# Four message-passing layers on one core: edge tiles of 128 in place of 125, and fewer near tiles

## The chip, the cores and the metric

The kernel runs on one core of a Trainium2 chip. Its time is the device time of one execution in microseconds. A core has five engines that matter here: TensorE (PE; its weight loads are listed apart as PEld), VectorE (DVE), ScalarE (ACT), GpSimd (POOL), and SyncE (SP), which issues most of the transfers. They run their own instruction streams and meet by semaphores.

## The reference

The graph has 3125 nodes with 16 features and 100,000 edges, sorted by destination. Four layers follow each other; each takes h = relu(layernorm(x)) and adds its result to x:

```
L0:  w_edge = relu(edge_attr_16 @ W1 + b1) @ W2 + b2        (16 x 16 per edge)
     msg = h[src] @ w_edge; out = relu(batchnorm(sum over dst + h @ root + bias))
L1:  msg = silu(sum_ij h[dst]_i * edge_attr_8_j * W[i,j,:]) @ W_lin, summed over src,
     then a second tensor product with the node's own features
L2:  two relational convolutions: msg = (h[src] @ W[edge_type]) / count(dst, edge_type),
     summed over dst; then log_softmax
L3:  out = in_degree^-1/2 * sum over dst of (h * out_degree^-1/2)[src]
```

Everything is float32. The kernel carries a float32 value through bfloat16 matmuls as three bfloat16 parts whose sum is the value.

## The kernel before

**Tiling.** Edges lie on partitions. A tile is EP = 125 edges, one on each of 125 partitions; T = 8 tiles are a chunk, and 100 chunks are all edges. Edge number p * 800 + c * 8 + t is partition p, chunk c, tile t, so each load of a chunk takes one piece of consecutive values per partition. Five phases run over all chunks in turn: l0, l1, l2a, l2b and l3, with short stages on the nodes between them. Chunks alternate between two buffers (s = 0, 1).

**Summing by node.** A chunk's messages are summed over their target node by matmuls into one accumulator `acc` [128, 392] that stays in PSUM for the whole phase. The target number is split in a high part (392 values) and a low part (8). DVE and ACT make a one-hot row of 392 for each edge (`one_hot`, L1206 on DVE, L866 and L879 on ACT), and DVE multiplies the three parts of the message by the one-hot of the low part (`stationary`, L1234). L600 is the matmul: 3 parts for 8 tiles, 24 per chunk. In l1 eight more (L607) count out-degrees, in l0 eight more (L604) count edges by node and type.

**Far and near tiles.** The message of an edge needs a row of its other node. For most tiles of a chunk, the far ones, GpSimd gathers these rows from a table in HBM: one indirect DMA per tile (L584), each with 125 row numbers, into `gathered`. The last tiles of a chunk, the near ones, get them without a gather. The node rows lie in SBUF as three bfloat16 parts on 125 partitions of 25 nodes each (`node_parts`). DVE makes a one-hot of the partition for each near edge (L1300, from `near_key`, which SyncE broadcasts to 125 partitions, L443), PE multiplies (L757, six matmuls per tile, 13 and 12 nodes wide), and DVE halves the row of 25 nodes four times by conditional copies (L1321) until one node's row is left. In l1 and l2 DVE then forms the outer product with the edge attributes or the type's one-hot (L1355), PE turns it (L765), ACT copies it (L979), and PE multiplies it by the weights (L773). `NEAR_OF` gives the near tiles of a chunk: none in l0, 3 in l1, 4 in l2a, l2b and l3. The far tiles are the rest of the eight: 8, 5, 4, 4, 4.

In l1 a far tile costs DVE a product of its 128-wide table row with the edge attributes (L1434) and three folds (L1432, L1445). The near tiles' edge attributes are loaded once in l0, for all chunks (`near_ea8`, L509, 1.17 MB in pieces of 96 bytes); the far tiles' come per chunk (`ea8`, L471).

**Order.** Every engine's order is written out by hand. For a chunk of a near phase DVE does the chunk's body (up to `stationary`), then `is_lo` of the next (L1187), then `near_finish` of the chunk after that, with the key comparisons of the third inside it. PE does 12 of its 24 sums, turns the outer product of two chunks ahead, 6 sums, the near rows of three chunks ahead, 6 sums, and the messages of two ahead; in l3 the near rows come after all sums. POOL starts the gathers of a chunk when its row numbers have arrived and DVE has read the rows of two chunks before (L577, L580). SP loads row numbers when the gathers of two chunks before have landed (L430), and the fields when ACT's distances and DVE's last use of two chunks before are done (L464, L465), then the near keys of two chunks ahead (L474).

**Start.** SP loads the edge lists src, dst and type (L376 to L378, 390 KB each), DVE and ACT make eight integer fields per edge from them, and SP stores them to HBM (L408, 3 MB), from where each phase reads them back by chunk.

Of the kernel before, what the change touches and what calls it, by code (L numbers as in the profile page):

```python
# [27 lines left out]
LO = 8  # L28
# [26 lines left out]
def build(nc, A, out):  # L55
    with ExitStack() as ctx:
# [161 lines left out]
        counts = ctx.enter_context(nc.psum_tensor("counts", [128, HI], F32))  # L218
        eaT_ps = ctx.enter_context(nc.psum_tensor("eaT_ps", [128, T, EP + 1], BF16))
        rows_ps = ctx.enter_context(nc.psum_tensor("rows_ps", [128, 3, 512], F32))  # L220
# [144 lines left out]
        WIDE_BANKS = (2, 3, 0)  # L365

        block = ctx.enter_context(nc.Block())


        @block.sync  # L370
        def _(sp):

            sp.wait_ge(ev("x_cleared"), 1)
            for p, l, n in as_nodes:
                sp.dma_start(x[p, l, :], A["x"][n].rearrange("(p l) f -> p l f", l=l.stop)).then_inc(ev("x_in"), 16)
            sp.dma_start(src[:], A["src"].rearrange("(p t) -> p t", p=EP)).then_inc(ev("edges_in"), 16)  # L376
            sp.dma_start(dst[:], A["dst"].rearrange("(p t) -> p t", p=EP)).then_inc(ev("edges_in"), 16)
            sp.dma_start(typ[:], A["edge_type_8"].rearrange("(p t) -> p t", p=EP)).then_inc(ev("edges_in"), 16)  # L378

# [8 lines left out]

            ea_d = A["edge_attr_16"].rearrange("(p c t) f -> p c (t f)", p=EP, t=T)
            ea8_d = A["edge_attr_8"].rearrange("(p c t) f -> p c (t f)", p=EP, t=T)  # L390
            rows_d = {ph: A[k].rearrange("(p c t) -> p c t", p=EP, t=T) for ph, k in (("l0", "src"), ("l1", "dst"), ("l3", "src"))}

            def load_ea(chunk, s):
                sp.dma_start(ea[:, s].rearrange("p t f -> p (t f)"),
                             ea_d[:, bass.ds(chunk, 1), :].rearrange("p c n -> p (c n)")).then_inc(ea_in[s], 16)

# [28 lines left out]

            def load_numbers(ph, chunk, pair, s):

                if later(chunk, 2):

                    sp.wait_ge(S[ph]["rows_in"][s], 16 * far(ph, s) * pair)  # L430
                if ph in rows_d:
                    rows = rows_d[ph][:, bass.ds(chunk, 1), :]
                else:
                    rows = meta_d[:, bass.ds(chunk, 1), SRC_KEY * T:(SRC_KEY + 1) * T]
                sp.dma_start(row_numbers[:, s, :], rows.rearrange("p c n -> p (c n)")).then_inc(numbers_in[s], 16)

            def load_near_keys(ph, chunk, s):
# [5 lines left out]
                sp.dma_start(near_key[:, s, 0:n], near_key_d[bass.ds(chunk, 1), at:at + n].to_broadcast([NEAR_NP, n])  # L443
                             ).then_inc(near_key_in[s], 16)

            def load_near_nodes(ph, into):
# [12 lines left out]
            def stream_near(ph):  # L459
                def body(chunk, pair, s):  # L460
                    load_numbers(ph, chunk, pair, s)
                    if later(chunk, 2):

                        sp.wait_ge(distances_ready, before(ph) + chunk - 1)  # L464
                        sp.wait_ge(S[ph]["step"], done(ph, FIELDS_READ[ph], chunk - 2))  # L465

                        sp.sem_inc(ev("chunks_begun"), 1)
                    sp.dma_start(fields[:, s].rearrange("p k t -> p (k t)"),
                                 meta_d[:, bass.ds(chunk, 1), :].rearrange("p c n -> p (c n)")).then_inc(fields_in[s], 16)
                    if ph == "l1":  # L470
                        sp.dma_start(ea8[:, s].rearrange("p t f -> p (t f)"),  # L471
                                     ea8_d[:, bass.ds(chunk, 1), :].rearrange("p c n -> p (c n)")).then_inc(ea8_in[s], 16)
                    if follows(chunk, 2):
                        load_near_keys(ph, chunk + 2, s)  # L474
                near_chunks(sp, body)

            def stream_l0():
                ph = "l0"

                def body(chunk, pair, s):  # L480
                    if later(chunk, 2):
                        load_numbers(ph, chunk, pair, s)

                        sp.wait_ge(ea_split, 2 * (chunk - 2) + 1)
                        load_ea(chunk, s)
# [29 lines left out]
                with sp.Fori((2 + LO) // 2, PAIRS) as pair:  # L515
                    for s in range(2):
                        body(2 * pair + s, pair, s)

# [76 lines left out]
        def _(pe):  # L595
# [147 lines left out]
            turn_h("l1")  # L743
            pe.wait_ge(ev("diagonals_in"), 16 * (8 * LO + 4))
            wide("l1", "msg")
# [97 lines left out]
        def _(act):  # L843
# [59 lines left out]

            act.wait_ge(ev("edges_in"), 48)
            act.copy(fields_all[:, :, TYPE, :].bitcast(F32), typ[:].rearrange("p (c t) -> p c t", t=T)
# [151 lines left out]
        def _(dve):  # L1057
# [49 lines left out]

            dve.wait_ge(ev("edges_in"), 48)
            for n in range(2):
# [23 lines left out]

            dve.wait_ge(ev("edges_in"), 48)

# [170 lines left out]
            def near_finish(ph, chunk, pair, s, following=True):  # L1306
# [43 lines left out]
                if ph == "l1":  # L1350
                    dve.tensor_copy(near_inverse[:, s, 0:count], rows[:, :, 0, F:ROW1])
                    factor = near_ea8[:, bass.ds(chunk, 1), :].rearrange("p c (t r) -> p (c t) r", t=NEAR1)[:, NEAR1 - count:]
                else:
# [240 lines left out]
```

## Time and profile before

| | |
|---|---|
| median of 3 runs | 4559.57 us (4553.13 to 4559.76) |
| the profiled execution | 4555.6 us, its span 4553.4 us |
| PE | 4339.6 us busy, 95% |
| PEld | 3261.8 us, 72% |
| DVE | 4121.4 us, 91% |
| ACT | 3235.6 us, 71% |
| POOL | 3284.9 us, 72% |
| DMA queues, share of 16 engines | GpSimd's 10.1%, SyncE's 7.8% |

Busy times are unions over the span of one execution. The end of a matmul is modelled, so a busy PE is not one at its peak. A gather's time on POOL ends when the transfer has been handed over, not when the rows have landed. "Issue" as what ended an idle time means that the engine waited for nothing that the profile shows.

### The profile page before, as it was taken

How to read it: one execution, taken by the hardware profiler on the slowest of the kernel's cores; microseconds unless marked ns; L12 is line 12 of the kernel's file. 1: busy time of each engine (PE TensorE's matmuls, PEld its weight loads, DVE VectorE, ACT ScalarE, POOL GpSimd, SP SyncE). 2: the span in 40 equal slices, each digit the busy share in tenths (PEclk: the TensorE clock that was granted, in tenths of full speed). 3: DMA queues.
4: the chain of work that ended last, by engine and by line, in shares of the span. 5: the costliest groups of instructions: out<-in, count | busy, mean ns of one | idle time of the engine just before them, and what ended most of it. 6: DMA issues, size and time to landing. Idle time of an engine off the chain costs nothing.

```text
span 4553.4 us, 107759 instructions
## 1 busy us (share of the span) xinstructions
PE 4339.6 (95%) x30477; PEld 3261.8 (72%) x30477; DVE 4121.4 (91%) x11864; ACT 3235.6 (71%) x5359; POOL 3284.9 (72%) x2515
## 2 busy tenths in 40 slices
PE   4999999999997999999979999998999999799998
PEld 3777777777775777777747777776777777566665
DVE  5999999999997999999969999997999998888887
ACT  3777777777774777777737777775777777677776
POOL 4888888888883777777727777775777775688886
PEclk8999999999998999999989999999999999899999
DMA  3111111111111222222211111111111111111111
GB/s 72 21 17 18 17 18 17 18 18 18 18 17 40 61 59 61 59 60 60 59 37 27 27 28 27 27 28 39 27 28 28 26 28 23 30 31 31 30 31 24
DMA packets 336556, 148.67 MB, mean 33 GB/s; under 512 B 250040, under 2 KB 322532, under 8 KB 336392
## 3 DMA queue, kind: packets, MB, share of 16 engines
q0 software_dynamic: 104000, 59.31, 10.1%
q1 hardware_dynamic: 232517, 88.88, 7.8%
q8 instruction: 19, 0.31, 0.0%
q14 instruction: 20, 0.16, 0.0%
HBM read 135.45 MB, written 9.80 MB: 32 GB/s over the span
## 4 chain that ended last, share of the span: by engine, by line
PE 81%; DVE 10%; issue 5%; ACT 2%; DMA 1%; SPq 1%; DVEq 0%; POOL 0%; POOLq 0%; ACTq 0%
PE acc L600 37%; PE rows_ps L757 16%; PE rows_ps L693 7%; PE bank L773 5%; PE bank L693 4%; PE counts L607 3%; PE eaT_ps L765 3%; DVE raw L1258 2%; PE rows_ps L681 2%; DVE stationary L1234 2%; PE eaT_ps L669 1%; DVE one_hot L1206 1%; PE counts L604 1%; DVE rows_ps L1321 1%; ACT stack L928 1%
## 5 line engine op out<-in xcount | busy, mean ns | idle before, releaser
L600 PE MATMUL acc<-one_hot,stationary 125*128 125x392 bf16 x12000 | 2335.4, 329 | 39.5 <-DVE stationary L1234 35.1
L584 POOL DMA_INDIRECT gathered<-table_l,row_numbers x1200 | 1607.3, 1339 | 461.1 <-issue 349.1
L600 PEld LDWEIGHTS acc<-one_hot,stationary 125*128 125x128 bf16 x12000 | 1157.3, 100 | 709.0 <-DVE stationary L1234 49.9
L866 ACT ACTIVATE distances<-count_hi,fields 125x392 bf16<-125x392 f16 (+1 forms) x2500 | 1227.5, 560 | 0.0
L1234 DVE TENSOR_TENSOR stationary<-mask,parts 125x1024 bf16<-125x1024 bf16 x1500 | 943.3, 683 | 0.3 <-ACT mask L851 0.2
L851 ACT CAST mask<-is_lo 125x1024 bf16<-125x1024 f32 x500 | 523.1, 1046 | 447.3 <-DVE is_lo L1187 393.5
L584 POOL DMA_INDIRECT fields_all<-table_l,row_numbers x500 | 646.3, 1293 | 259.6 <-issue 114.8
L1206 DVE TENSOR_SCALAR one_hot<-count_hi,fields 125x392 bf16<-125x392 f16 x2300 | 734.4, 341 | 13.5 <-issue 13.5
L1321 DVE COPY_PREDICATED rows_ps<-near_bits_now,rows_ps 125x320 f32<-125x320 int8 (+3 forms) x1600 | 579.7, 362 | 162.6 <-PE rows_ps L757 118.6
L584 POOL DMA_INDIRECT gathered<-table_l2a,row_numbers x400 | 512.7, 1282 | 282.6 <-DVE parts L1216 119.4
L757 PE MATMUL rows_ps<-node_parts,h1T 125*125 125x192 bf16 (+1 forms) x7200 | 678.3, 252 | 27.0 <-DVE node_parts L1285 19.6
L757 PEld LDWEIGHTS rows_ps<-node_parts,h1T 125*125 125x125 bf16 x7200 | 660.8, 138 | 56.0 <-DVE node_parts L1285 19.8
L584 POOL DMA_INDIRECT gathered<-table_l2b,row_numbers x400 | 512.6, 1282 | 242.0 <-DVE parts L1216 119.2
L879 ACT ACTIVATE one_hot<-distances,ones 125x1568 bf16<-125x1568 bf16 (+1 forms) x400 | 675.0, 1687 | 6.6
L979 ACT COPY h1T<-eaT_ps 128x500 f32<-128x500 f32 (+1 forms) x300 | 162.7, 542 | 431.5 <-PE eaT_ps L765 431.5
L1258 DVE TENSOR_REDUCE raw<-product 125x32 f32<-125x512 f32 x400 | 395.6, 1010 | 0.0
L693 PE MATMUL rows_ps<-w,h1T 128*125 128x256 f32 x1600 | 385.9, 384 | 9.7 <-DVE product L1251 8.1
L693 PE MATMUL bank<-w,h1T 128*125 128x256 f32 x1600 | 379.7, 380 | 0.0
L693 PEld LDWEIGHTS rows_ps<-w,h1T 128*125 128x125 f32 x1600 | 294.7, 189 | 59.1 <-DVE product L1251 9.5
L693 PEld LDWEIGHTS bank<-w,h1T 128*125 128x125 f32 x1600 | 302.0, 189 | 45.8
L1300 DVE TENSOR_SCALAR h1T<-near_key,node_key 125x500 bf16<-125x500 f16 (+1 forms) x800 | 319.3, 400 | 12.3 <-DMA near_key<-near_keys_by_chunk 12.3
L941 ACT ACTIVATE h1T<-rows_ps,b 128x500 f32<-128x500 f32 x400 | 249.7, 676 | 90.1 <-PE rows_ps L681 90.0
(213 smaller groups left out, 4706.6 us busy)
## 6 DMA issues: line engine op xcount, KB each, us to landing
near_key<-near_keys_by_chunk SPq DMA_DIRECT2D x300, 122.1 KB
gathered<-table_l,row_numbers POOLq DMA_INDIRECT x1200, 2.8
fields<-edge_fields SPq DMA_DIRECT2D x500, 31.2 KB
near_key<-near_keys_by_chunk SPq DMA_DIRECT2D x100, 91.6 KB
fields_all<-table_l,row_numbers POOLq DMA_INDIRECT x500, 3.5
gathered<-table_l2a,row_numbers POOLq DMA_INDIRECT x400
gathered<-table_l2b,row_numbers POOLq DMA_INDIRECT x400
ea<-in_edge_attr SPq DMA_DIRECT2D x100, 62.5 KB
```

Of the source, the lines that this page charges most:

```text
L584: pool.indirect_dma_start(out=gathered[ph][:, s, t, :], in_=table[ph], out_offset=None, in_offset=bass.IndirectOffsetOnAxis(ap=row_numbers ...
L600: mm = pe.matmul(acc[:, :], stationary[:, s, k, t, :, :].rearrange("p a b -> p (a b)"), one_hot[:, s, t, :], start=first and t == 0 and k ...
L693: mm = pe.matmul(bank[2 + q % 2][0:EP, j * HID:(j + 1) * HID], h1T[:, half, t * EP:(t + 1) * EP], w2[:, half, :], start=half == 0, stop=ha ...
L757: mm = pe.matmul(near_rows_ps[ph][:, t, 0:end - first, :].rearrange("p a f -> p (a f)"), near_one_hot[:, g, t * EP:(t + 1) * EP], parts_of ...
L851: act.copy(mask[:, s].rearrange("p t a f -> p (t a) f"), is_lo[:, s].rearrange("p t a -> p (t a)")[:, :, None].to_broadcast([EP, T * LO, F ...
L866: ins = act.activation(distances[:, i * n:(i + 1) * n], count_hi[:, 0:n], ACT.Abs, scale=-1.0, bias=fields[:, s, k, t:t + 1].bitcast(F32))
L879: act.activation(into, distances[:, 0:into.shape[1]], ACT.Relu, scale=-1.0, bias=ones[0:EP, 0:1]).then_inc(scalar_hot, 1)
L1206: dve.tensor_scalar(one_hot[:, s, t, :], count_hi[:, :], scalar_field(s, hi_field[ph], t), None, ALU.is_equal)
L1234: ins = dve.tensor_tensor(stationary[:, s, k], mask[:, s], source[:, s, :, k * F:(k + 1) * F][:, :, None, :].to_broadcast([EP, T, LO, F]), ...
L1258: dve.tensor_reduce(raw[:, s, 2 * q:2 * q + 2, :], product[:, q % 2].rearrange("p t i o -> p t o i"), AX.X, ALU.add).then_inc(products_sum ...
L1300: ins = dve.tensor_scalar(near_one_hot[:, g, 0:n], near_key[:, s, 0:n], node_key[:, g:g + 1], None, ALU.is_equal)
L1321: return dve.copy_predicated(into, chosen, source)
```

## The change

A tile is 128 edges. 100,000 is not a multiple of 1024, so there are 98 chunks, 352 places more than edges. The edges are read through two views that overlap: the first 54 chunks are the first 55,296 edges, partition-major; the last 44 start 352 edges earlier, so that on partition 0 they repeat edges. Those are taken out at the start: on partition 0 DVE sets the source to an unused slot and the destination to a number beyond all one-hots. `near_key` is loaded to 128 partitions and read on 125. `NEAR_OF` becomes 2 in l1, 3 in l2a and l2b, 4 in l3, so the far tiles are 6, 5, 5 and 4. `near_ea8` holds two chunks and is loaded per chunk in l1, behind the near keys and on their semaphore. SP's loops are split where the view changes.

```diff
-EP, T = 125, 8
+EP, T = 128, 8
 E = 100000
-TILES = E // EP
-CHUNKS = TILES // T
+CHUNKS = -(-E // (EP * T))
+TILES = CHUNKS * T
 PAIRS = CHUNKS // 2
-NEAR_OF = {"l0": (0, 0), "l1": (3, 3), "l2a": (4, 4), "l2b": (4, 4), "l3": (4, 4)}
+PADDING = EP * TILES - E
+WHOLE = CHUNKS - PADDING // T
+WHOLE_EDGES = EP * WHOLE * T
+NEAR_OF = {"l0": (0, 0), "l1": (2, 2), "l2a": (3, 3), "l2b": (3, 3), "l3": (4, 4)}
...
-        near_key = sb("near_key", [NEAR_NP, 2, NEARS * EP], F16)
+        near_key = sb("near_key", [128, 2, NEARS * EP], F16)
...
-        near_ea8 = sb("near_ea8", [EP, CHUNKS, NEAR1 * RELATIONS])
+        near_ea8 = sb("near_ea8", [EP, 2, NEAR1, RELATIONS])
...
+        def near_keys_in_by(ph, pair):
+            return 32 * (pair + 1) if ph == "l1" else 16 * (PAIRS + chunks_before(ph) // 2 + pair + 1)
...
+        def by_rows(v):
+            names = "(p c t) f -> p c t f" if len(v.shape) == 2 else "(p c t) -> p c t"
+            return (v[0:WHOLE_EDGES].rearrange(names, p=EP, t=T),
+                    v[WHOLE_EDGES - PADDING:].rearrange(names, p=EP, t=T))
...
+            for into, k in ((src, "src"), (dst, "dst"), (typ, "edge_type_8")):
+                whole, ragged = by_rows(A[k])
+                sp.dma_start(into[:, 0:WHOLE * T], whole.rearrange("p c t -> p (c t)")).then_inc(ev("edges_in"), 16)
+                sp.dma_start(into[:, WHOLE * T:], ragged.rearrange("p c t -> p (c t)")).then_inc(ev("edges_in"), 16)
...
+                if ph == "l1":
+                    if later(chunk, 2):
+                        sp.wait_ge(near_outers, chunk - 1)
+                    sp.dma_start(near_ea8[:, s].rearrange("p t r -> p (t r)"),
+                                 rows_of(ea8_d, chunk, ragged, (T - NEAR1) * RELATIONS)).then_inc(near_key_in[s], 16)
...
-                            sp.dma_start(near_ea8[:], ea8_d[:, :, (T - NEAR1) * RELATIONS:]).then_inc(ev("diagonals_in"), 16)
...
+            dve.memset(src[0:1, WHOLE * T:], SLOTS - 1)
+            link(dve.memset(dst[0:1, WHOLE * T:], SLOTS))
...
-                        dve.wait_ge(near_key_in[s], 16 * (chunks_before(ph) // 2 + pair + 1))
-                    ins = dve.tensor_scalar(near_one_hot[:, g, 0:n], near_key[:, s, 0:n], node_key[:, g:g + 1], None, ALU.is_equal)
+                        dve.wait_ge(near_key_in[s], near_keys_in_by(ph, pair))
+                    ins = dve.tensor_scalar(near_one_hot[:, g, 0:n], near_key[0:NEAR_NP, s, 0:n], node_key[:, g:g + 1], None, ALU.is_equal)
```

## Rows read from the trace of the kernel before

**Rows 1.** Windows in L0, L1, L2a, L3: columns in the first line.

```profile
core 0: us, PE busy (x) PEld busy (x) DVE busy (x) ACT busy (x) POOL busy (x), PEclk, DMA share, GB/s
600.00:1200.00 600.00, 595.06 (x3424) 435.07 (x3423) 579.41 (x1263) 452.72 (x812) 490.04 (x361) 1.00 0.13 18
1500.00:2300.00 800.00, 800.00 (x5557) 605.52 (x5556) 757.32 (x2548) 604.33 (x1038) 610.76 (x472) 1.00 0.27 60
2450.00:3050.00 600.00, 600.00 (x4967) 476.78 (x4966) 559.37 (x1817) 437.08 (x662) 424.23 (x331) 1.00 0.16 27
3950.00:4450.00 500.00, 476.47 (x3737) 345.52 (x3736) 449.46 (x1401) 386.72 (x623) 405.18 (x312) 1.00 0.20 31
```

**Rows 2.** GpSimd's groups, windows L0, L1, L2a, L3: xcount | busy, mean ns | idle before.

```profile
L584 POOL DMA_INDIRECT gathered<-table_l,row_numbers x361 | 491.1, 1360 | 110.0 <-issue 96.6 <-DVE rest L1219 13.1 <-DVE msg L1271 0.3
L584 POOL DMA_INDIRECT fields_all<-table_l,row_numbers x472 | 611.7, 1296 | 189.4 <-issue 107.8 <-DVE parts L1225 74.0 <-DMA row_numbers<-in_dst 7.6
L584 POOL DMA_INDIRECT gathered<-table_l2a,row_numbers x331 | 424.4, 1282 | 176.6 <-DVE parts L1216 101.1 <-issue 62.5 <-DMA row_numbers<-edge_fields 13.1
L584 POOL DMA_INDIRECT gathered<-table_l,row_numbers x312 | 406.3, 1302 | 95.1 <-issue 82.6 <-DVE is_lo L1187 11.9 <-DMA row_numbers<-in_src 0.6
```

**Rows 3.** Chain of waits, L1: start, us, what.

```profile
1492.74 2.29 PE rows_ps L757 x18
1501.23 2.29 PE rows_ps L757 x18
```

**Rows 4.** Timeline of PE, L2a: start, us, what.

```profile
2609.33 0.59 PE L765 MATMUL eaT_ps<-ident,fields_all 125*128 125x125 f32 x4
2616.59 0.59 PE L765 MATMUL eaT_ps<-ident,fields_all 125*128 125x125 f32 x4
```

**Rows 5.** Timeline of GpSimd, L0.

```profile
705.27 1.21 POOL L584 DMA_INDIRECT gathered<-table_l,row_numbers  x1 [0.30 <-issue]
```

**Rows 6.** Waits in the windows of L2a and L3: us in total, times, longest.

```profile
DVE rows_ps L1321 <- PE rows_ps L757: 26.6, 74, 0.5
...
PE acc L600 <- DVE stationary L1234: 23.5, 39, 0.6
```

**Rows 7.** Timeline of PE, L3.

```profile
4107.09 4.15 PE L600 MATMUL acc<-one_hot,stationary 125*128 125x392 bf16 x24 [0.60 <-DVE stationary L1234]
4111.08 2.22 PE L757 MATMUL rows_ps<-node_parts,h1T 125*125 125x208 bf16 x24
```

**Rows 8.** DVE's groups by form, whole span: xcount | busy, mean ns | idle before.

```profile
L1321 DVE COPY_PREDICATED rows_ps<-near_bits_now,rows_ps 125x360 f32<-125x360 int8 x100 | 53.1, 531 | 7.5 <-PE rows_ps L757 7.1 <-ACT near_bits_now L987 0.4
L1321 DVE COPY_PREDICATED rows_ps<-near_bits_now,rows_ps 125x72 f32<-125x72 int8 x100 | 23.8, 238 | 14.5
L1300 DVE TENSOR_SCALAR h1T<-near_key,node_key 125x500 bf16<-125x500 f16 x600 | 252.2, 421 | 8.3 <-DMA near_key<-near_keys_by_chunk 8.3
L1300 DVE TENSOR_SCALAR h1T<-near_key,node_key 125x375 bf16<-125x375 f16 x200 | 67.1, 336 | 4.0 <-DMA near_key<-near_keys_by_chunk 4.0
```

**Rows 9.** DMA queues, windows L2a and L1: packets, MB, share.

```profile
q1 hardware_dynamic: 32370, 13.37, 8.5%
q0 software_dynamic: 10566, 3.03, 7.8%
...
q0 software_dynamic: 37698, 32.62, 18.2%
```

**Rows 10.** SyncE in L1: its longest wait, and its timeline.

```profile
SPq L465 <- ACT distances L866: 557.5, 90, 6.4
...
1698.81 0.26 SPq L443 DMA_DIRECT2D near_key<-near_keys_by_chunk  x1
```

**Rows 11.** Chain of waits, start.

```profile
4.86 16.51 DMA stage<-in_edge_type
...
47.49 11.03 DMA gathered<-table_l,row_numbers
...
74.51 21.58 SPq L511
```

More of the change, by code:

```diff
@@ L387, in _, with rows_of, load_ea @@
                 sp.dma_start(b1[:, a:a + 1], A["L0_gnn_b1"][a * 128:(a + 1) * 128][:, None]).then_inc(ev("w1_in"), 16)
[L389 to L393, printed above, removed]
+            ea_d = [v.rearrange("p c t f -> p c (t f)") for v in by_rows(A["edge_attr_16"])]
+            ea8_d = [v.rearrange("p c t f -> p c (t f)") for v in by_rows(A["edge_attr_8"])]
+            rows_d = {ph: by_rows(A[k]) for ph, k in (("l0", "src"), ("l1", "dst"), ("l3", "src"))}
+            def rows_of(views, chunk, ragged, first=0):
+                view, at = (views[1], chunk - WHOLE) if ragged else (views[0], chunk)
+                return view[:, bass.ds(at, 1), first:].rearrange("p c n -> p (c n)")
+            def load_ea(chunk, s, ragged=False):
                 sp.dma_start(ea[:, s].rearrange("p t f -> p (t f)"),
-                             ea_d[:, bass.ds(chunk, 1), :].rearrange("p c n -> p (c n)")).then_inc(ea_in[s], 16)
+                             rows_of(ea_d, chunk, ragged)).then_inc(ea_in[s], 16)
             for s in range(2):
@@ L424, in later_copies, with load_numbers @@
                     sp.dma_start(bd[k][rows, lo, :, :], A[w].rearrange("r i o -> i r o")).then_inc(ev("diagonals_in"), 16)
-            def load_numbers(ph, chunk, pair, s):
+            def load_numbers(ph, chunk, pair, s, ragged=False):
                 if later(chunk, 2):
@@ L431, in load_numbers, with load_near_keys @@
                 if ph in rows_d:
-                    rows = rows_d[ph][:, bass.ds(chunk, 1), :]
+                    rows = rows_of(rows_d[ph], chunk, ragged)
                 else:
-                    rows = meta_d[:, bass.ds(chunk, 1), SRC_KEY * T:(SRC_KEY + 1) * T]
-                sp.dma_start(row_numbers[:, s, :], rows.rearrange("p c n -> p (c n)")).then_inc(numbers_in[s], 16)
-            def load_near_keys(ph, chunk, s):
+                    rows = meta_d[:, bass.ds(chunk, 1), SRC_KEY * T:(SRC_KEY + 1) * T].rearrange("p c n -> p (c n)")
+                sp.dma_start(row_numbers[:, s, :], rows).then_inc(numbers_in[s], 16)
+            def load_near_keys(ph, chunk, s, ragged=False):
                 if later(chunk, 2) or ph != "l1":
@@ L459, in stream_near, with body @@
             def stream_near(ph):
-                def body(chunk, pair, s):
-                    load_numbers(ph, chunk, pair, s)
+                def body(chunk, pair, s, ragged):
+                    load_numbers(ph, chunk, pair, s, ragged)
                     if later(chunk, 2):
@@ L471, in body @@
                         sp.dma_start(ea8[:, s].rearrange("p t f -> p (t f)"),
-                                     ea8_d[:, bass.ds(chunk, 1), :].rearrange("p c n -> p (c n)")).then_inc(ea8_in[s], 16)
+                                     rows_of(ea8_d, chunk, ragged)).then_inc(ea8_in[s], 16)
                     if follows(chunk, 2):
-                        load_near_keys(ph, chunk + 2, s)
-                near_chunks(sp, body)
+                        load_near_keys(ph, chunk + 2, s, chunk + 2 >= WHOLE if isinstance(chunk, int) else ragged)
+                for chunk in range(2):
+                    body(chunk, 0, chunk, False)
+                with sp.Fori(1, WHOLE // 2 - 1) as pair:
+                    for s in range(2):
+                        body(2 * pair + s, pair, s, False)
+                for chunk in range(WHOLE - 2, WHOLE):
+                    body(chunk, chunk // 2, chunk % 2, False)
+                with sp.Fori(WHOLE // 2, PAIRS - 2) as pair:
+                    for s in range(2):
+                        body(2 * pair + s, pair, s, True)
+                for chunk in range(CHUNKS - 4, CHUNKS):
+                    body(chunk, chunk // 2, chunk % 2, True)
             def stream_l0():
                 ph = "l0"
-                def body(chunk, pair, s):
+                def body(chunk, pair, s, ragged=False):
                     if later(chunk, 2):
-                        load_numbers(ph, chunk, pair, s)
+                        load_numbers(ph, chunk, pair, s, ragged)
                         sp.wait_ge(ea_split, 2 * (chunk - 2) + 1)
-                        load_ea(chunk, s)
+                        load_ea(chunk, s, ragged)
                     if later(chunk, 2):
@@ L514, in stream_l0 @@
                         later_copies(chunk - 2)
-                with sp.Fori((2 + LO) // 2, PAIRS) as pair:
-                    for s in range(2):
-                        body(2 * pair + s, pair, s)
+                for first, end in (((2 + LO) // 2, WHOLE // 2), (WHOLE // 2, PAIRS)):
+                    with sp.Fori(first, end) as pair:
+                        for s in range(2):
+                            body(2 * pair + s, pair, s, end == PAIRS)
             def store_table(ph, stage, where):
@@ L743, in _ @@
             turn_h("l1")
-            pe.wait_ge(ev("diagonals_in"), 16 * (8 * LO + 4))
+            pe.wait_ge(ev("diagonals_in"), 16 * (8 * LO + 3))
             wide("l1", "msg")
@@ L1351, in near_finish @@
                     dve.tensor_copy(near_inverse[:, s, 0:count], rows[:, :, 0, F:ROW1])
-                    factor = near_ea8[:, bass.ds(chunk, 1), :].rearrange("p c (t r) -> p (c t) r", t=NEAR1)[:, NEAR1 - count:]
+                    factor = near_ea8[:, s, NEAR1 - count:]
                 else:
```

14 lines of the change are left out of this document (6 added, 8 removed).

## The prediction

> **What bounds the kernel now.** I read the table of engines first, with one window in each phase [rows 1]. In the tensor-product phase (L1) and the first relational one (L2a; L2b repeats it) TensorE is busy for all of the window and VectorE for 93 to 95%; in L0 PE has 99% and DVE 97%, in the last phase (L3) 95% and 90%. The granted clock is 1.00 in all of them. Then the period of a chunk. From the gathers in a window: 361 of 8 a chunk in 600 us are 13.30 us in L0, 312 of 4 in 500 us are 6.41 in L3 [rows 2]. From equal pieces: 1492.74 and 1501.23 are 8.49 us in L1 [rows 3], 2609.33 and 2616.59 are 7.26 in L2 [rows 4]. One hundred chunks each, L2 twice, are 1330 + 849 + 726 + 726 + 641 = 4272 of the 4555.6 us of the profiled execution; the rest is the start, the node stages and the end.
>
> GpSimd is busy for 71 to 82% of the windows [rows 1] and yet near its limit. After each gather stand 0.30 us that end by nothing: 110.0/361 in L0, 95.1/312 in L3, with 1.36 and 1.30 us for the gather itself. Eight and four of these are 13.3 and 6.4 us, the whole period. In L1 five are 8.0 of 8.49, in L2 four are 6.35 of 7.26, and there GpSimd waits for DVE as well [rows 2]. An undisturbed gather is 1.21 us [rows 5]; what goes beyond comes beside DVE's work. But in L0 and L3 GpSimd is not what others wait for: in L3 the wait of the matmul engine is for DVE's stationary, 23.5 us over 78 chunks, and no gather is in the list [rows 6]. I read L3 as a loop through PE and DVE.
>
> **Chunks.** 800 tiles in 100 chunks become 784 in 98; all that is paid per chunk is paid twice less in each phase. A row of a tile is a partition, so sums, masks and stationaries cost what they did. Columns that count edges grow from 125 to 128, in parts of the chunk only; I count 0 for them and at most 2.4% of the hidden layer's matmuls, under 0.1 us a chunk.
>
> **Near tiles, L1 from 3 to 2, L2 from 4 to 3.** PE: 24 matmuls of the sum take 3.99 us (4107.09 to 4111.08) [rows 7]. So in L2 four near tiles have the other 7.26 - 3.99 = 3.27, each 0.82, and PE needs 6.44 with three. L1 has 32 such matmuls, 5.32, and 3.17 for three near tiles; two leave 7.43.
>
> DVE: a conditional copy costs (531 - 238)/288 = 1.02 ns per element, a key comparison (421 - 336)/125 = 0.68 ns per column [rows 8]. L1 loses 120 + 96 + 48 + 24 elements in its four copies (-0.29), 119 columns in each of two comparisons (-0.16), and 128 elements of the outer product (-0.13, by the same 1.02). It gains one far tile: 128 elements in the product, 64 and 32 in the folds, 16 in the sum, +0.25. Together -0.33. L2 loses 192 elements of copies (-0.20), 116 columns twice (-0.16) and 128 of the outer product (-0.13): -0.49. DVE's own need today: busy 757.3/800 of 8.49 is 8.04 us in L1, 559.4/600 of 7.26 is 6.77 in L2 [rows 1]. In L2 it idles 0.32 us a chunk for PE's rows (26.6 us, 83 chunks [rows 6]), so without PE it needs 6.94, and 6.45 after; I take 6.55, as the loop with PE (6.44) is as long. In L1 it idles 0.45, and I put half on PE: 8.26 - 0.33 = 7.93, taken as 8.0. DVE is late next, PE behind it by 0.1 to 0.6 us. Bounds: today's busy time less the edit, 7.7 and 6.3, and today's period less nothing, 8.49 and 7.26.
>
> **Gathers.** Each near tile less is a gather more: 6 a chunk in L1, 5 in L2. This decides the sign. Means are 1296 and 1282 ns where the undisturbed one is 1.21, so DVE adds 5 x 0.086 = 0.43 and 4 x 0.072 = 0.29 us a chunk [rows 2, 5]; I keep 0.4 and 0.3. At 1.21 us GpSimd would need 6 x 1.515 + 0.4 = 9.49 us in L1 and 5 x 1.515 + 0.3 = 7.88 in L2, above both old periods. What does a gather of 128 rows cost? No row has one, but the queues show how 125 are issued [rows 9]. SyncE's three loads of a chunk in L2 make 32370/83 = 390 packets, 3 x (125 + 5). A gather in L2 moves 3.03 MB/331 = 9154 bytes, of which 125 rows of 64 are 8000. The other 1154 are 288 pieces of 4 bytes: 16 for a semaphore and 272 more, about 11 x 25. In L1 it is 32.62 MB/472 = 69.1 KB for rows of 544 (68.0): the same 1.1 KB. I read it as five DMA engines with 25 rows each and eleven with 25 dummies, some 400 entries for 125 rows. 128 divides by 16, and 16 x 8 = 128 entries do.
>
> The Trainium skill, "DMA: Bandwidth & Descriptors", section "Why a DMA increments its semaphore by 16 and not by 1", has the rule: a DMA uses the largest number of engines up to 16 that divides its slowest dimension, so 5 for 125 and 16 for 128. By that rule, the trace agrees (390 packets).
>
> Bounds of the new gather: 1.21 us if the entries cost nothing (1.24 if time goes with rows), and 1.21 x 8/25 = 0.39 if they are all of it. No row has another count, so I take the middle, 0.8: half of it fixed. Below a threshold the value does not matter: 6 (g + 0.305) + 0.4 reaches 8.0 at g = 0.96, 5 (g + 0.305) + 0.3 reaches 6.55 at 0.945. Up to there DVE sets both phases. That half of the old cost is in the entries is my choice; it is enough that a third is (1.21 x (0.67 + 0.33 x 0.32) = 0.94).
>
> The Trainium skill speaks against so low a value: the section "Latency and other measured facts" of the same page gives about 1 us for what the software path spends on making descriptors. By it, as an estimate from that page, L1 would be 98 x 8.23 and L2 98 x 6.83, and the kernel some 4340 us; the trace's 1.21 stands above the page's figure for 125 rows, and no run here yet shows 128. In rows this is rival B below.
>
> **SyncE.** In L1 the near edge attributes come per chunk now, one issue more of about 0.26 us with a wait on an outer product of two chunks before, long done. The queue waits 557.5/90 = 6.2 us per chunk for ACT's distances, and behind the new issue stand only the row numbers of the next chunk, so I count 0; without that cover it is 98 x 0.26 = 25 us [rows 10]. Loads that now use 16 engines land earlier; in the steady state nobody waits for them.
>
> **Start.** On the chain stand 16.51 us for the edge lists, 11.03 for the first gathers, which share the queues with the 3 MB store of the fields, and 21.58 in which the store of near keys is stuck behind the load of near attributes that the change removes [rows 11]. With an ordinary landing of 2 us left in each, 14 + 9 + 21 = 44 us is the upper bound, 0 the lower (part of each is covered by the node work). I take 25.
>
> **Sum** against 4555.6: L0 2 x 13.30, -27; L1 98 x 8.0 = 784 for 849, -65; L2 98 x 6.55 = 642 for 726, -84 twice; L3 2 x 6.41, -13; start -25. That is -298, 4258. The median of the runs is 4 us above the profiled one: 4262.
>
> **Rivals.** A, slower: the gather stays at 1.21, because its time is fixed and not in the entries. GpSimd then sets L1 (98 x 9.49 = 930, +81) and L2 (98 x 7.88 = 772, +46 twice); less the 65 of L0, L3 and start it is +108, 4668. It turns slower where 588 g - 631 + 980 g - 1094 passes 65, at g = 1.14. For it: rows of 64 and of 544 bytes took the same time. Against it: two thirds of the entries go. Chance 0.13.
> B, between: four fifths fixed, g = 1.05. L1 98 x 8.53 = 836 (-13), L2 98 x 7.08 = 693 (-33 twice), -65: -144, 4416. Chance 0.17.
> C, more: GpSimd's shorter spans disturb DVE less, so the loops of L0 and L3 give half of the 0.30 us that PE waits in L3 (196 x 0.15 = 29) and L1 and L2 0.1 a chunk more (29): 4204. Chance 0.15.
> The forecast has 0.55.
>
> **Range.** 4200 to 4440 holds the forecast, B and C and leaves A out; the forecast's own is 4220 to 4310. Faster by over 0.2% (9 us, about what can be told from no change) 0.86, within it 0.02, slower 0.12, which is nearly all of A.
>
> **What would show it.** A gather under 0.95 us; its queue without the 4-byte dummies; DVE at 97% or more in L1 and L2 and PE idle before DVE's stationary; periods of 8.0 and 6.55, and 13.3 and 6.4 as before in L0 and L3; no 21 us issue at the start. GpSimd without a gap in L1 and L2 and DVE waiting for gathered rows would show A or B. A gather of over 1.0 us makes me wrong.

## The result, and the profile after

The changed kernel took 5332.49 us (median of 4 runs, 5289.03 to 5351.86), beside 4559.65 for the kernel before in the same set of runs: ratio 1.169, 95% interval 1.161 to 1.176, and 25% above the forecast. The profiled execution has 5330.2 us and a span of 5328.3. As the experiments will show, one fact belongs beside it: run again beside a kernel before of 4553.4 us, the same program took 4247.7, ratio 0.932 (0.930 to 0.934). What follows compares these two traces of one program. I call them the long run and the short run.

Windows of the long run, one in each phase (columns as in [rows 1]):

```profile
200.00:1300.00 1100.00, 964.91 (x5401) 694.60 (x5399) 896.04 (x1980) 716.99 (x1280) 587.73 (x568) 0.99 0.09 15
1700.00:2500.00 800.00, 635.23 (x3950) 403.74 (x3948) 628.82 (x2135) 495.45 (x872) 509.14 (x474) 0.97 0.25 55
2750.00:3500.00 750.00, 597.10 (x4087) 418.62 (x4086) 516.07 (x1767) 410.68 (x641) 390.22 (x401) 0.91 0.13 19
4700.00:5200.00 500.00, 422.08 (x3088) 285.79 (x3087) 363.11 (x1161) 320.72 (x518) 265.88 (x257) 0.97 0.15 26
```

Windows of the short run, the same four phases:

```profile
500.00:1100.00 600.00, 587.13 (x3383) 440.06 (x3427) 565.20 (x1262) 455.11 (x812) 374.68 (x362) 1.00 0.11 18
1450.00:2150.00 700.00, 644.55 (x4260) 430.40 (x4258) 664.45 (x2302) 536.26 (x938) 544.20 (x512) 1.00 0.32 68
2300.00:2850.00 550.00, 549.97 (x4326) 411.99 (x4324) 536.14 (x1869) 429.85 (x679) 420.40 (x425) 1.00 0.20 27
3650.00:4150.00 500.00, 495.94 (x3853) 349.92 (x3851) 460.63 (x1448) 398.17 (x644) 330.55 (x322) 1.00 0.20 32
```

The last count before the clock is GpSimd's gathers: 8, 6, 5 and 4 a chunk. So the period of a chunk is 8 x 1100/568 = 15.5 us in L0, 10.1 in L1, 9.35 in L2 and 7.8 in L3 in the long run, and 13.26, 8.20, 6.47 and 6.21 in the short one. In the long run no engine is as full as in the short one (PE has 79 to 88%, GpSimd 52 to 64%), and the granted clock falls to 0.91 in L2. What the engines wait for is seen in the list of waits of the whole span (us in total, times, longest), first the long run:

```profile
DVE rows_ps L1361 <- remote: 616.1, 147, 6.4
...
PEld acc L638 <- issue: 294.5, 1014, 4.5
ACT h1T L1017 <- remote: 253.4, 76, 11.9
...
PE bank L811 <- issue: 190.9, 152, 7.0
```

Of the four the short run has only the second, with 8.0 us; it stands here below that run's largest "remote" wait:

```profile
ACT h1T L979 <- remote: 54.1, 97, 0.6
...
PEld acc L638 <- issue: 8.0, 37, 0.8
```

"Issue" and "remote" mean that no instruction of this core released the one that waits. One such stretch, in the timeline of the long run (start, us, engine, line; rows between these are left out):

```profile
3010.09 1.16 PE L638 MATMUL acc<-one_hot,stationary 128*128 128x392 bf16 x6
3010.36 0.14 SPq L464 DMA_DIRECT2D near_key<-near_keys_by_chunk  x1
3011.18 0.26 DVE L1227 TENSOR_TENSOR is_lo<-count_key,fields 128x64 f32<-128x64 f32 x1
3011.18 0.95 POOL L622 DMA_INDIRECT gathered<-table_l2a,row_numbers  x1 [0.30 <-issue]
3011.81 0.18 PE L811 MATMUL bank<-relation_weights,h1T 128*128 128x16 f32 x1 [0.48 <-issue]
3012.39 0.19 ACT L1025 COPY near_bits_now<-near_bits 128x12 int8 x1
3012.53 0.19 PEld L811 LDWEIGHTS bank<-relation_weights,h1T 128*128 128x128 f32 x1 [1.19 <-issue]
3013.25 0.18 PE L811 MATMUL bank<-relation_weights,h1T 128*128 128x16 f32 x1 [1.26 <-issue]
3013.43 2.15 ACT L904 ACTIVATE distances<-count_hi,fields 128x392 bf16<-128x392 f16 x4
3013.68 0.95 POOL L622 DMA_INDIRECT gathered<-table_l2a,row_numbers  x1 [0.30 <-issue]
3013.96 0.19 PEld L811 LDWEIGHTS bank<-relation_weights,h1T 128*128 128x128 f32 x1 [1.24 <-issue]
3014.68 0.18 PE L811 MATMUL bank<-relation_weights,h1T 128*128 128x16 f32 x1 [1.25 <-issue]
3016.11 0.42 PE L811 MATMUL bank<-relation_weights,h1T 128*128 128x16 f32 x2 [1.25 <-issue]
3016.47 0.41 DVE L1361 COPY_PREDICATED rows_ps<-near_bits_now,rows_ps 128x240 f32<-128x240 int8 x1 [5.03 <-remote]
```

Read the PE and PEld rows together: one instruction at 3011.81, 3012.53, 3013.25, 3013.96, 3014.68, that is one every 0.72 us, though each takes 0.2 and waits for nothing. DVE stands still for 5.03 us, of which 3.9 come after the last thing that it waited for (`near_bits_now`, done at 3012.58), and SyncE's register instructions beside it are 0.7 us apart as well. GpSimd keeps its pace, a gather every 1.25 us, and the stretch ends 1.5 us after the last gather of the chunk. ACT shows nothing of the 0.72 us: its four `distances` come 0.51 us apart, as in the short run.

I counted such places over whole traces: pairs of successive instructions of PE, PEld or SyncE that start 0.695 to 0.750 us apart, the second waiting for nothing (and, on PE and PEld, starting 0.3 us or more after the first has ended). I call them slow pairs, and a place with several of them a slow stretch. The long run has 417 slow pairs, the short run 0, the kernel before 1. Of the 417, 412 begin while a gather is on GpSimd or less than 1 us after one; of the whole time 74% is like that, so the tie to the gathers is strong, but as a count it is no proof.

The difference of the spans, 1082 us, is 314 us of PE busy time (4318.2 against 4004.6) and 769 us of PE idle time. The busy part is mostly clock: TensorE's granted clock was at its lower level (1.2 GHz) for 660 us of the long run and for 152 of the short one. Where work takes twice as long, 508 us more are at most 254 us of PE's 314. The mean matmul of the sum took 345 ns, against 330. After the stretch above such matmuls start 0.327 us apart, before it 0.165. So the stalls cost twice, by themselves and by the lower clock behind them.

### The profile page after: what moved, and what is told of

Same layout as the page of the kernel before. It is cut to its first block, busy times and chain, and to the rows that moved or that the text cites. A ratio compares the mean times of both kernels' runs of the same rounds, so it can differ in the third digit from the quotient of the medians.

```text
span 5328.3 us, 100613 instructions
## 1 busy us (share of the span) xinstructions
PE 4318.2 (81%) x27224; PEld 2970.4 (56%) x27224; DVE 3930.9 (74%) x11632; ACT 3131.7 (59%) x5253; POOL 2805.9 (53%) x2759
## 4 chain that ended last, share of the span: by engine, by line
PE 34%; DVE 22%; issue 17%; another core or an unknown queue 16%; ACT 8%; DVEq 2%; DMA 1%; ACTq 0%; POOL 0%; SPq 0%; POOLq 0%
PE acc L638 12%; DVE stationary L1274 6%; PE rows_ps L731 6%; PE bank L731 5%; PE rows_ps L795 4%; ACT distances L904 4%; DVE rows_ps L1361 3%; DVE one_hot L1246 3%; PE eaT_ps L707 2%; PE rows_ps L719 2%; PE eaT_ps L803 1%; DVE raw L1298 1%; DVE h1T L1340 1%; PE counts L642 1%
## 5 line engine op out<-in xcount | busy, mean ns | idle before, releaser
L638 PE MATMUL acc<-one_hot,stationary 128*128 128x392 bf16 x11760 | 2459.2, 345 | 265.1 <-DVE stationary L1274 111.5
L638 PEld LDWEIGHTS acc<-one_hot,stationary 128*128 128x128 bf16 x11760 | 1168.8, 103 | 1052.1 <-issue 294.5
L904 ACT ACTIVATE distances<-count_hi,fields 128x392 bf16<-128x392 f16 (+1 forms) x2450 | 1198.7, 558 | 0.0
L1361 DVE COPY_PREDICATED rows_ps<-near_bits_now,rows_ps 128x240 f32<-128x240 int8 (+7 forms) x1568 | 514.1, 328 | 715.9 <-remote 616.1
L1274 DVE TENSOR_TENSOR stationary<-mask,parts 128x1024 bf16<-128x1024 bf16 x1470 | 933.9, 689 | 8.8 <-ACT mask L889 8.8
L889 ACT CAST mask<-is_lo 128x1024 bf16<-128x1024 f32 x490 | 511.4, 1044 | 526.9 <-DVE is_lo L1227 205.6
L1246 DVE TENSOR_SCALAR one_hot<-count_hi,fields 128x392 bf16<-128x392 f16 x2254 | 680.0, 324 | 70.0 <-remote 56.8
L917 ACT ACTIVATE one_hot<-distances,ones 128x1568 bf16<-128x1568 bf16 (+1 forms) x392 | 660.4, 1685 | 6.5
L795 PE MATMUL rows_ps<-node_parts,h1T 125*128 125x208 bf16 (+1 forms) x5880 | 592.0, 258 | 82.2 <-ACT gathered L1030 57.2
L795 PEld LDWEIGHTS rows_ps<-node_parts,h1T 125*128 125x128 bf16 x5880 | 536.8, 102 | 142.2 <-ACT gathered L1030 67.5
```

Of the source, the lines that this page charges most:

```text
L638: mm = pe.matmul(acc[:, :], stationary[:, s, k, t, :, :].rearrange("p a b -> p (a b)"), one_hot[:, s, t, :], start=first and t == 0 and k ...
L795: mm = pe.matmul(near_rows_ps[ph][:, t, 0:end - first, :].rearrange("p a f -> p (a f)"), near_one_hot[:, g, t * EP:(t + 1) * EP], parts_of ...
L889: act.copy(mask[:, s].rearrange("p t a f -> p (t a) f"), is_lo[:, s].rearrange("p t a -> p (t a)")[:, :, None].to_broadcast([EP, T * LO, F ...
L904: ins = act.activation(distances[:, i * n:(i + 1) * n], count_hi[:, 0:n], ACT.Abs, scale=-1.0, bias=fields[:, s, k, t:t + 1].bitcast(F32))
L917: act.activation(into, distances[:, 0:into.shape[1]], ACT.Relu, scale=-1.0, bias=ones[0:EP, 0:1]).then_inc(scalar_hot, 1)
L1246: dve.tensor_scalar(one_hot[:, s, t, :], count_hi[:, :], scalar_field(s, hi_field[ph], t), None, ALU.is_equal)
```

## The experiments

Kernels that ran together, a set, did so on one chip, and the kernel before ran beside each set. The record gives a chip number with every set but the first. It does not say whether a number means the same chip each time:

```
set  chip  before us  kernels (us)
1    -     4559.65    changed 5332
2    2     4554.1     near only 4798, edges only 4425, keys125 4247, loads5 4248
3    15    4584.4     changed again 5522, before with keys128 4582
4    7     4580.4     one memset 5527, one load 5514, keys126 5546, keys128 in L3 5528
5    15    4553.4     changed, third time 4248, loads5 4247, edges only 4426, gathers125 4709
6    7     4559.7     loads5 5503, gathers125 4706
7    2     4559.6     edges only 5113, spaced 5332
```

Sets 2 and 5 are short ones, sets 1, 3, 4, 6 and 7 long ones. The expectations below, from the third time of the changed kernel on, speak of fast and slow chips. The record does not bear that out: number 15 stands with long set 3 and short set 5, and number 2 with short set 2 and long set 7. The letters are theories, each said in the expectation where it first comes.

**Set 2: parts of the change.** Near only is the kernel before with `NEAR_OF` of the changed one.

> The kernel before, with tiles of 125 edges, and only the near tiles changed: two in L1, three in L2. In the changed kernel stretches of 1 to 6 us recur in which TensorE, VectorE and SyncE all take about 0.7 us for each instruction; the trace of before has none. Theory L (SyncE's transfers on 16 DMA engines instead of 5 bring them) and theory G (gathers on 16 engines do) both expect no such stretch here, and a kernel that waits for GpSimd in L1 and L2, at 1.21 us a gather: 6 x 1.515 + 0.4 = 9.5 us and 5 x 1.515 + 0.3 = 7.9 us a chunk, together 4560 + 100 x (1.0 + 2 x 0.6) = about 4790 us. Theory N (the added gathers of L1 and L2 bring the stretches, whatever the tile) expects them in L1 and L2, and over 4900 us.

4797.5 us, ratio 1.053 (1.051 to 1.055), one slow pair. L1 ran at 6 x 1.602 = 9.6 us a chunk and L2 at 5 x 1.591 = 7.95 (spacing of its gathers): GpSimd sets them. With 125 rows a gather, the near tiles alone cost 5%. (The expectation says of the changed kernel that VectorE too takes 0.7 us an instruction; no pair of DVE's shows that, only gaps like the one above.)

Edges only is the changed kernel with `NEAR_OF` of before.

> The changed kernel, with tiles of 128 edges, and the near tiles as before: three in L1, four in L2. Theories L and G (transfers or gathers on 16 DMA engines bring the stretches of 0.7 us an instruction) expect them in all phases, L0 at 15.3 us and L3 at 7.8 us a chunk as in the changed kernel, L1 near 10.3 and L2 near 9, in all 5250 to 5450 us. Theory N (added gathers) expects L1 and L2 free of them and 98 chunks at the old periods or below: under 4800 us.

4425.3 us, ratio 0.972 (0.970 to 0.973), two slow pairs. All theories that expected stretches here were wrong, as it seemed. Next the near keys:

```diff
-        near_key = sb("near_key", [128, 2, NEARS * EP], F16)
+        near_key = sb("near_key", [NEAR_NP, 2, NEARS * EP], F16)
-    ... near_key_d[bass.ds(chunk, 1), at:at + n].to_broadcast([128, n])
+    ... near_key_d[bass.ds(chunk, 1), at:at + n].to_broadcast([NEAR_NP, n])
```

> The changed kernel with one edit: the near keys are broadcast to the 125 partitions that are read, not to 128, so this transfer of L1, L2 and L3 (the largest that SyncE issues) goes through 5 DMA engines again. Theory L (SyncE's transfers on 16 engines) expects shorter or fewer stretches in L1, L2 and L3, none gone in L0 (which has no such transfer, 15.3 us a chunk), in all 4800 to 5150 us. Theory G (gathers) expects no difference, 5330 us within 1%.

4247.0 us, ratio 0.933 (0.931 to 0.934). It looked like the cause found, but L0 was at 13.3 us too, where the two programs do not differ in an instruction. Loads5 adds to it, with the counts of the waits doubled:

```diff
+            def load_rows(into, rows, into_sem):
+                for p in (slice(0, 125), slice(125, 128)):
+                    sp.dma_start(into[p], rows[p]).then_inc(into_sem, 16)
```

> The changed kernel, with every streamed transfer of SyncE (row numbers, fields, edge attributes, near attributes) split into 125 and 3 partitions, and the near keys on 125: at most 5 DMA engines for each. The gathers keep their 128 rows on 16 engines. Theory L expects no stretches of 0.7 us an instruction and the periods that I forecast, 13.3, 8.0, 6.55 and 6.4 us: 4260 to 4400 us with twice the issues on SyncE. Theory G (the gathers on 16 engines bring the stretches) expects 5250 to 5450 us.

4248.0 us, ratio 0.933 (0.931 to 0.934).

**Sets 3 and 4: is it the near keys?**

> The changed kernel itself, unaltered. The kernel with the near keys on 125 partitions took 4247 us and lost the slow stretches in L0 too, where neither kernel loads near keys and the instructions are the same. Theory K (the 128-partition near keys are the cause, by whatever way) expects 5290 to 5350 us again. Theory P (the 5332 us belong to something outside the instructions, such as the chip or where the program lay that time) expects another time, near 4250 us.

5522.0 us, ratio 1.207 (1.203 to 1.210): the long time again, longer than K had it and far from P's 4250. For the kernel before with near keys on 128 partitions:

> The kernel before, with tiles of 125 edges, and one edit: the near keys are broadcast to 128 partitions (three more than are read), so through 16 DMA engines. Theory K in its simple form (a broadcast over 16 engines brings stretches of 0.7 us an instruction) expects them in L1, L2 and L3, and 4900 to 5300 us. If it takes more than that edit (the version with 128 partitions, three and four near tiles, and tiles of 128 took 4425 us without them), or by theory P, it stays within 0.5% of 4555 us.

4582.3 us, ratio 1.000 (0.999 to 1.001). It has 26 slow pairs, all on SyncE, where the kernel before has 1, and they cost nothing: it takes what the kernel before takes in the same set. Then four neighbours of the changed kernel: one `dve.memset` more; one `sp.dma_start` of 128 x 32 bytes more; the near keys `to_broadcast([126, n])`; and `p = 128 if ph == "l3" else NEAR_NP` for the near keys.

> The changed kernel with one VectorE memset of 128 elements more, at the start, before anything that lasts. Not one transfer differs. The changed kernel took 5332 and 5522 us; with the near keys on 125 instead of 128 partitions it took 4247, and 4582 became nothing else when the kernel before got the same edit. Theory K (the 128-partition near keys cost the time in themselves, together with fewer near tiles) expects 5300 to 5550 us. Theory P (the slow form is one of arrangement, and any small difference in the program can end it) expects near 4250 us. Theory R (what counts is how SyncE's transfers stand in the queues of the DMA engines) expects 5300 to 5550 us, as K.

> The changed kernel with one SyncE transfer more, at the start: 128 partitions of 32 bytes into a tile that nothing reads. Theory K expects 5300 to 5550 us. Theory P expects near 4250 us, and theory R too (the transfer shifts every later one in the queues of all 16 engines).

> The changed kernel with the near keys on 126 partitions. 126 divides by 14, so the broadcast should use 14 DMA engines of 9 rows each (the queue's packets will show it), nearly as wide as 128 on 16. Theory K, if width is the matter, expects 5200 us or more. If all 16 engines being alike in their load is the matter (R), or by P, it is near 4250 us.

> The changed kernel with the near keys on 125 partitions in L1 and L2 and on 128 in L3 alone. Theory K expects the slow stretches in L3 alone, 98 x 1.4 us: about 4380 us. Theory R expects all phases to be as the kernel with 125, L0 to L2 included, 4247 us, or, if what is left over from one execution slows the next, all of them slow, over 5000 us. Theory P expects 4250 us.

5526.6, 5513.7, 5545.9 and 5528.4 us, ratios 1.206, 1.204, 1.207 and 1.208 (all intervals between 1.199 and 1.216), with 489 to 522 slow pairs. (In keys126 SyncE's queue has 1568 packets fewer than in the changed kernel, four for each of 392 loads of near keys, as two engines less would make.) The last decides against K: with the near keys on 125 partitions in L1 and L2 these were as slow as ever, and so was L0. P and R fell too. What the six long and the three short results of tiles of 128 had in common was only their set.

**Set 5: the same programs in another set.**

> The changed kernel, unaltered, a third time, as the control for the three kernels that run beside it on the same chip. Theory S (the chip decides: some chips are slow for kernels of this kind) expects either near 4250 us with the others at their fast times, or 5300 to 5550 us with others slow as well. Theory K (the near keys on 128 partitions) expects 5300 to 5550 us on every chip.

4247.7 us, ratio 0.932 (0.930 to 0.934). K, and my reading of keys125, are gone: the set decides. Theory S says more, that the chip does, and that is not shown. By its number this is the chip of set 3, where the same program took 5522 us some twenty minutes before; if the number means one chip, S is wrong, and what decides is something that changes with time.

> The kernel with every streamed transfer of SyncE on at most 5 DMA engines, byte for byte as before, when it took 4248 us. Theory K expects 4248 us within 0.5% again. Theory S expects over 5000 us if the unaltered changed kernel is slow beside it. If S holds and this one is yet fast, SyncE's loads on 16 engines are what a slow chip punishes (theory L).

4247.0 us, no different from the changed kernel, so it tells nothing here.

> Tiles of 128 with the near tiles of before (three and four), byte for byte the kernel that took 4425 us. If the unaltered changed kernel is slow beside it: theory L and theory G (the gathers on 16 engines are what a slow chip punishes) expect over 5200 us, theory N (only the added gathers of L1 and L2 matter) 4400 to 4500 us.

4426.0 us, ratio 0.972 (0.970 to 0.974), as in set 2. Gathers125 is the changed kernel with the edit below, and with the tiles `gathered0` and `gathered2` cleared once at the start. It leaves out the rows of three edges in 128, so it is no kernel to use:

```diff
-                            out=gathered[ph][:, s, t, :], in_=table[ph], out_offset=None,
-                            in_offset=bass.IndirectOffsetOnAxis(ap=row_numbers[:, s, t:t + 1], axis=0),
+                            out=gathered[ph][0:125, s, t, :], in_=table[ph], out_offset=None,
+                            in_offset=bass.IndirectOffsetOnAxis(ap=row_numbers[0:125, s, t:t + 1], axis=0),
```

> The changed kernel with each gather reading 125 of its 128 rows (the edges of partitions 125 to 127 get no rows, so this leaves out 2.3% of the gathering), so on the 5 engines and dummies of before, at 1.21 us each. SyncE's loads keep 16 engines. GpSimd then sets L1 and L2, as my rival A had it: 98 x 9.5 and 98 x 7.9 us, about 4670 us. Theory G expects that and no stretch of 0.7 us an instruction, also where the unaltered kernel is slow. Theory L expects the stretches and 5300 us or more there.

4708.8 us, ratio 1.033 (1.027 to 1.040), near the 4668 of rival A.

**Sets 6 and 7: what a long set punishes.** This needs a long set, and set 6 was one.

> All streamed transfers of SyncE on at most 5 DMA engines, the gathers on 16, unaltered. If the kernel before takes under 4557 us beside it, the chip is of the fast kind, and it repeats 4247. If it takes 4560 or more, the chip is of the slow kind: theory L (SyncE's wide transfers are what it punishes) expects 4250 to 4300 us, theory G (the wide gathers) and theory N (the added gathers, of whatever width) 5300 us or more.

5503.1 us, ratio 1.207 (1.203 to 1.210), 758 slow pairs, 753 of them during a gather or less than 1 us after one (71% of the time is like that). Loads over five engines do not help: theory L falls.

> Each gather reads 125 of its 128 rows (2.3% of the gathering is left out), SyncE's transfers keep 16 engines. Where the kernel before takes 4560 us or more beside it: theory G expects 4700 to 4750 us, theory L 5300 us or more, with stretches of 0.7 us an instruction.

4705.5 us beside it, ratio 1.032 (1.028 to 1.036), as in set 5, and no slow pair. It is not that slower gathers merely hide the stretches: L0, which they do not bound, runs at 8 x 1.663 = 13.3 us a chunk, as in the short run, where the long run has 15.5. The waits of gathers125 in a stretch of L2 (2500 to 3100):

```profile
DVE msg L1556 <- DMA gathered<-table_l2a,row_numbers: 94.0, 74, 1.5
POOL gathered L625 <- issue: 90.2, 296, 0.3
```

The first row is an ordinary wait for rows, and no "remote" wait is in that stretch. The gather itself, in its timeline and in that of the long run:

```profile
3001.49 1.21 POOL L625 DMA_INDIRECT gathered<-table_l2a,row_numbers  x1 [0.30 <-issue]
3003.00 1.21 POOL L625 DMA_INDIRECT gathered<-table_l2a,row_numbers  x1 [0.30 <-issue]
```

```profile
3011.18 0.95 POOL L622 DMA_INDIRECT gathered<-table_l2a,row_numbers  x1 [0.30 <-issue]
3012.44 0.94 POOL L622 DMA_INDIRECT gathered<-table_l2a,row_numbers  x1 [0.30 <-issue]
```

So one edit, 125 rows a gather for 128, takes all slow stretches away in that set, while it keeps the tile of 128 in every other instruction, SyncE's wide loads and the number of gathers. Theory G is shown as to the place: it is the gathers. More than one thing differs in them, though. Those of 128 rows spread the rows over 16 engines, where those of 125 have them on five and 4-byte dummies on eleven, and they come every 1.25 us instead of 1.51. Set 7 asked which.

> Tiles of 128 with three and four near tiles, unaltered (4425 us twice, beside a kernel before of 4554). Where the kernel before takes 4557 us or more, the chip is of the slow kind, and theory G (wide gathers) expects 5100 us or more, L0 at 15 us a chunk or more, as in the changed kernel. Only if the added gathers were needed for the loss would it stay near 4430 us.

5112.6 us, ratio 1.121 (1.115 to 1.128), against 4425 and 4426 in sets 2 and 5: the loss does not need the added gathers. Then the changed kernel with a memset behind each gather (its tile `pause` is left out here):

```diff
+                        pool.wait_ge(ev("paused"), pauses + far(ph, s) * chunk + t)
+                        pool.sem_inc(ev("chunks_begun"), 1)
+                        pool.memset(pause[:], 0.0).then_inc(ev("paused"), 1)
```

> The changed kernel with a small GpSimd memset after each gather, so that the gathers of a chunk start some 1.5 us apart, as those of 125 rows do, but still use 16 engines. On any chip GpSimd then sets L1 and L2, near 9.4 and 7.8 us a chunk, 4650 to 4800 us. On a chip of the slow kind: if the pace is what it punishes, that is all, and no stretches of 0.7 us an instruction; if the width is, they stay and it takes 5300 us or more.

5332.3 us, ratio 1.170 (1.164 to 1.176), 858 slow pairs. This looks like a verdict for width, and is not one: the memset went mostly into the 0.30 us between the gathers, and the median spacing rose only from 1.25 to 1.33 us, not to 1.5. The kernel did not do what it was built for. A look into its trace leans to width: 125 of its gathers are the third in a row with starts 1.49 us or more apart, and 35 slow pairs fall behind them, about as many per gather as in all (858 for 2744). But 113 of these 125 had a closer gather just ahead, so width or pace stays open.

## Why the prediction was wrong, point by point

The prediction has a sum that is nearly right for the short sets, and nothing in it for the long ones, and it was measured in a long one. In set 5, beside a kernel before of 4553.4 us, its steps stand as follows.

**Chunks.** 98 chunks of 13.26 and 6.21 us in L0 and L3 (forecast 13.3 and 6.4). L3 fell by 0.2 us a chunk, which I gave only to rival C.

**Near tiles.** L1 8.20 for a forecast of 8.0, L2 6.47 for 6.55. But the reason was half wrong: I had DVE late next, at 97% or more. DVE has 95% in L1 and 97% in L2 (second windows above). In both, GpSimd has no gap but the 0.30 us behind each gather, as its groups in the short run's windows of L1 and L2a show, answering to [rows 2]:

```profile
L622 POOL DMA_INDIRECT fields_all<-table_l,row_numbers x512 | 545.3, 1065 | 156.1 <-issue 156.1
```

```profile
L622 POOL DMA_INDIRECT gathered<-table_l2a,row_numbers x425 | 421.3, 991 | 129.9 <-issue 103.4 <-DVE msg L1553 12.8 <-DVE rest L1259 12.8
```

6 x (545.3 + 156.1)/512 = 8.22 us is the whole period of L1, and 5 x 551.2/425 = 6.49 that of L2. This is the mechanism of rival B, at a lower price.

**Gathers.** The undisturbed one is 0.95 us where I took 0.8. The bounds, 0.39 and 1.21, hold it. The dummies are gone: the queue shows

```profile
q0 software_dynamic: 13573, 3.50, 9.0%
```

for 425 gathers, 8.2 KB each where it was 9.15 [rows 9], 128 rows of 64 bytes and a semaphore. By 0.95 alone the threshold (0.96 and 0.945) is just reached. What makes L1 20 us longer than forecast is what a gather takes beyond that: its mean is 1.065 us, so 6 x 0.115 = 0.69 us a chunk, where I had kept 0.4, measured on five gathers and not scaled to six. In L2 it is 5 x 0.041 = 0.2 for my 0.3, and costs nothing. The Trainium skill, "DMA: Bandwidth & Descriptors", section "Latency and other measured facts", gives about 1 us to the first byte on the software path, as the time that GpSimd takes to make the descriptors. The traces show 0.95 us for 128 rows and 1.21 for 125, which one fixed figure does not tell apart.

**Start.** L1's first gather came at 1391 us, where it was 1451 before: 60 us for L0 and the start, forecast 27 + 25. The 21 us issue [rows 11] is gone from the chain.

**Sum.** 4247.7 for a forecast of 4262, in that set, and some of that is luck. From the first gather of a phase to that of the next, L1 lost 44 us for a forecast 65, L2 91 and 82 for 84 each, and L3 with the end 30 for 13: two errors of about 20 us cancel. GpSimd's price of a gather of 125 rows was right too: near only and gathers125 took 4798 and 4709, the latter for a rival A of 4668.

**The step that failed** stands in two places. "Gathers" prices what a gather costs GpSimd and, by the difference of 1296 and 1282 to 1210 ns, what DVE's work costs the gather. What the gather costs the other engines is not priced at all, that is, it stands at nothing without a reason, and rival C had it only as a gain. And under "SyncE" I wrote "Loads that now use 16 engines land earlier; in the steady state nobody waits for them": true of the loads (loads5 took 4247 and 4248 us in the short sets and 5503 in a long one, about what the changed kernel took), but the gathers of 128 rows have a cost that I set to nothing. In set 1 it is some 2.2 us a chunk in L0, 1.9 in L1, 2.9 in L2 and 1.6 in L3, 98 x (2.2 + 1.9 + 2 x 2.9 + 1.6) = 1127 us, in fair agreement with the 1082 between the spans. That L0 lost too, where a chunk has 8 gathers as before, should have told me at once that neither near tiles nor near keys were the cause; it took until set 4.

The trace of before could not have shown it: no row there has a gather of 128 rows. But a form of transfer that no row shows has an unknown effect on others as well as an unknown price, and I bounded only the price. The chance of a slower kernel, 0.12, was rival A's alone.

**What stays open.** Whether the width or the pace of the gathers counts. What makes a set long: the kernel before tells the sets apart only by medians of 4553 and 4554 against 4560 to 4584 us, and single runs overlap (4553.1 in set 1, 4557.8 in set 5). The chip by its number does not, as the table shows. Where the program's tables lay in memory, and what else ran on the chip, is not on record and was not tried. And what the 0.72 us is: PE, its weight loads and SyncE are held to it, DVE has long gaps instead, and not every instruction is held (between the matmul at 3014.68 and the weight load at 3015.39 PE's queue took four loop instructions within 0.47 us). DMA packets are no longer than elsewhere (data packets of the gathers 98 ns on the mean in the long run's L2a, 107 in the short run's). All times come from recorded executions; whether the hold is there without the recording was not tried. No version here beats the kernel before in both kinds of set: the changed one is 7% faster in one and 17 to 21% slower in the other, edges only 3% faster and 12% slower.

## What to carry to other kernels

When a change makes a transfer take another form, bound what it does to the other engines' pace, not only what it costs its own queue; a form that the trace has never shown deserves a rival on the slow side. Before explaining a surprising time, run the same program again beside its control on another occasion: two kernels with small edits "cured" mine here only because they ran in another set. And if a stall is in a phase whose instructions did not change, look for what is shared, not for what was edited beside it.

## What was not expected of the hardware

A gather of 128 rows keeps GpSimd for 0.95 us and one of 125 rows for 1.21, though it fetches three rows more. In five of seven sets such gathers went with stretches in which PE, its weight loads and SyncE started one instruction in about 0.72 us and DVE stood still (up to 6.4 us in the long run); in the other two, programs with the same gathers have at most two slow pairs each. The kernel before, which gathers 125 rows, differs between these sets by 0.1 to 0.7%, so it gives no warning.
